# The polynomial of the norms' inverse root: from VectorE to GpSimd in a one-core transformer kernel

## What is computed

```python
def l2norm(t):
    return t / jnp.maximum(jnp.linalg.norm(t, axis=-1, keepdims=True), 1e-12)

def attn_layer(x, Wqkv, qs, ksc, Wo):
    q, k, v = jnp.split(x @ Wqkv, 3, -1)          # each to 16 heads of 64
    q, k = l2norm(q) * qs, l2norm(k) * ksc
    ...                                            # rotary tables on q and k
    out = local_attention(q, k, v)                 # softmax over two windows of 32
    return out @ Wo

def ffn_layer(x, g, bln, W1, b1, W2, b2):
    mu = x.mean(-1, keepdims=True)
    var = ((x - mu) ** 2).mean(-1, keepdims=True)
    xn = (x - mu) / jnp.sqrt(var + 1e-05) * g + bln
    ...
for i in range(DEPTH):                             # 6 layers
    x = attn_layer(shift_tokens(x), ...) + x
    x = ffn_layer(shift_tokens(x), ...) + x
```

## Time and profile before

| | before |
|---|---|
| median of 3 runs | 1721.71 us (1720.7 to 1721.73) |
| span of the profiled execution | 1725.8 us |
| TensorE busy | 1585.1 us, 92% |
| VectorE busy | 1446.8 us, 84% |
| ScalarE busy | 1117.1 us, 65% |
| GpSimd busy | 1069.6 us, 62% |

### The profile page before, as it was taken

How to read it: one execution, slowest core, us unless ns; L and a number is a source line. 1 busy time by engine, 2 the same in 40 slices (tenths; PEclk the granted TensorE clock), 3 DMA queues, 4 the chain that set the end, 5 groups by cost and what they waited for, 6 DMA issues and landing times.

```text
span 1725.8 us, 77157 instructions
## 1 busy us (share of the span) xinstructions
PE 1585.1 (92%) x32762; PEld 1278.6 (74%) x32763; DVE 1446.8 (84%) x3173; ACT 1117.1 (65%) x2014; POOL 1069.6 (62%) x1040
## 2 busy tenths in 40 slices
PE   4569999899999998999999999999999999999987
PEld 2247877777878777778777788777777777877874
DVE  8978988888889887888888889888888888888862
ACT  4346776667667666677666666666766666776663
POOL 3656766666666665667566567476576575665640
PEclk8589999999999999999999999999999999999998
DMA  2111110201111211110211111211111111011110
GB/s 86 31 44 49 40 49 25 77 24 48 44 37 37 65 36 38 41 49 28 67 34 48 41 37 40 61 37 52 38 40 40 49 49 44 29 47 44 33 46 13
DMA packets 41084, 75.06 MB, mean 43 GB/s; under 512 B 9472, under 2 KB 22568, under 8 KB 40744
## 3 DMA queue, kind: packets, MB, share of 16 engines
q1 hardware_dynamic: 40744, 70.12, 14.0%
HBM read 20.08 MB, written 2.10 MB: 13 GB/s over the span
## 4 chain that ended last, share of the span: by engine, by line
PE 75%; issue 9%; DVE 5%; ACT 4%; POOL 2%; ACTq 0%; DVEq 0%; POOLq 0%
PE bank L1359 8%; PE bank L1328 8%; PE bank L1465 8%; PE bank L1396 8%; PE wide L1436 7%; PE bank L1330 7%; PE bank L1329 7%; PE bank L1451 5%; PE bank L1529 4%; PE bank L1414 3%; PE bank L1385 2%; PE bank L1514 2%; PE bank L1515 1%; PE bank L1516 1%; PE bank L1476 1%
## 5 line engine op out<-in xcount | busy, mean ns | idle before, releaser
L864 POOL TENSOR_TENSOR qk<-qk,rnorm 128x512 f32<-128x512 f32 x384 | 401.8, 1046 | 351.0 <-DVE rnorm L1017 351.0
L856 POOL TENSOR_TENSOR qk<-qk,qk_sin 128x512 f32<-128x512 f32 x384 | 492.3, 1282 | 174.6 <-DVE qk_sin L978 174.5
L1180 ACT ACTIVATE squares<-bank 128x512 f32<-128x512 f32 x384 | 229.5, 598 | 152.6 <-DVE qk_sin L978 152.6
L988 DVE TENSOR_REDUCE norm<-squares 128x8 f32<-128x512 f32 x384 | 258.4, 678 | 30.7 <-ACT squares L1180 28.5
L1328 PE MATMUL bank<-w_hi,xs_hi 128*128 128x512 f32 x576 | 264.3, 459 | 12.3 <-ACT squares L1180 7.0
L971 DVE TENSOR_TENSOR qk<-bank,tables 128x512 f32<-128x512 f32 x384 | 261.6, 681 | 9.4 <-PE bank L1330 9.2
L978 DVE TENSOR_TENSOR qk_sin<-bank,tables 128x512 f32<-128x512 f32 x384 | 261.1, 680 | 0.6 <-POOL qk L856 0.6
L1330 PE MATMUL bank<-w_hi,xs_lo 128*128 128x512 f32 x576 | 230.3, 400 | 0.9 <-issue 0.9
L1329 PE MATMUL bank<-w_lo,xs_hi 128*128 128x512 f32 x576 | 229.2, 398 | 1.2 <-issue 1.1
L1359 PE MATMUL bank<-ident,qk 128*128 128x128 f32 x1536 | 226.5, 278 | 3.3 <-POOL qk L864 1.5
L1359 PEld LDWEIGHTS bank<-ident,qk 128*128 128x128 f32 x1536 | 181.0, 142 | 43.5 <-issue 5.0
(11 more groups left out here) (181 smaller groups left out, 2735.8 us busy)
## 6 DMA issues: line engine op xcount, KB each, us to landing
v<-v SPq DMA_DIRECT2D x96, 390.0 KB, 3.5
v<-v SPq DMA_DIRECT2D x72, 130.0 KB, 3.7
w_raw<-in_L_ffn_Wqkv SPq DMA_DIRECT2D x36, 256.0 KB, 3.9
w_o_s<-in_L_ffn_Wo SPq DMA_DIRECT2D x6, 512.0 KB, 5.9
w_raw<-in_L_ffn_W SPq DMA_DIRECT2D x6, 341.0 KB, 4.2
mix_x_nat<-in_L_attn_x SPq DMA_DIRECT2D x4, 256.0 KB, 3.5
w_raw<-x_res_scratch SPq DMA_DIRECT2D x4, 256.0 KB, 3.5
out<-w_raw SPq DMA_DIRECT2D x4, 256.0 KB, 3.1
```

What stands on the lines that cost most here:

```text
L856: pool.tensor_tensor(qk[:, g % 2, c, :], qk[:, g % 2, c, :], qk_sin[:, (QK_CHUNKS * g + c) % SINES, :], ALU.add).then_inc(added[c], 1)
L864: pool.tensor_tensor(view, view, rnorm[:, g % 2, c * HPC:(c + 1) * HPC].unsqueeze(2) .to_broadcast([P, HPC, DH]), ALU.mult).then_inc(norme ...
L988: dve.tensor_reduce(norm2[:, c * HPC:(c + 1) * HPC], squares[:, c % 2, :].rearrange("p (h d) -> p h d", d=DH), AX.X, ALU.add).then_inc(sum ...
```

## The change

The clamp and the seed stay on VectorE (`root_seed`, two instructions, the second raises the new semaphore `root_seeded`). The polynomial goes to GpSimd (`root`), at the start of its step, ahead of `normalise(step - 1, 3)`. GpSimd's three-input form is not used, so the seven instructions become ten: seven `tensor_tensor` and three `tensor_scalar`, with a semaphore wait between any two. The last raises `rooted`. `sum_squares` of chunk 0 now also waits for `rooted`, since it overwrites what the root reads.

```diff
+            chain = Chain(pool, late.pool_seq, late.pool_steps)
+            def root(g):
+                if not with_norms(g) and not with_var(g):
+                    return
+                x, y = norm2[:, root_cols(g)], rnorm[:, g % 2, root_cols(g)]
+                s, w = root_t[:, root_cols(g)], root_w[:, root_cols(g)]
+                pool.wait_ge(root_seeded, root_count(g))
+                chain(pool.tensor_tensor(s, x, y, ALU.mult))
+                chain(pool.tensor_tensor(w, s, y, ALU.mult))
+                chain(pool.tensor_scalar(s, w, 1.0, -10.0 / 3.0, ALU.mult, ALU.add))
+                chain(pool.tensor_tensor(s, s, w, ALU.mult))
+                chain(pool.tensor_scalar(s, s, 1.0, 5.0, ALU.mult, ALU.add))
+                chain(pool.tensor_tensor(y, s, y, ALU.mult))
+                chain(pool.tensor_tensor(s, x, y, ALU.mult))
+                chain(pool.tensor_tensor(w, s, y, ALU.mult))
+                chain(pool.tensor_scalar(w, w, -27.0 / 1024.0, 9.0 / 16.0, ALU.mult, ALU.add))
+                pool.tensor_tensor(y, w, y, ALU.mult).then_inc(rooted, 1)
...
+                root(step - 1)
                 normalise(step - 1, 3)
                 add(step - 1, 2)
...
                 dve.wait_ge(squared[c], g + 1)
+                if c == 0:
+                    need(dve, rooted, g)
...
                 seq(dve.tensor_scalar(x, x, 1e-24, None, ALU.max))
-                seq(dve.tensor_scalar(y.bitcast(I32), x.bitcast(I32), -0.5, float(0x5F3759DF), ALU.mult, ALU.add))
-                seq(dve.tensor_tensor(s, x, y, ALU.mult))
-                seq(dve.tensor_tensor(w, s, y, ALU.mult))
-                seq(dve.scalar_tensor_tensor(s, w, -10.0 / 3.0, w, ALU.add, ALU.mult))
-                seq(dve.scalar_tensor_tensor(y, s, 5.0, y, ALU.add, ALU.mult))
-                seq(dve.tensor_tensor(s, x, y, ALU.mult))
-                seq(dve.scalar_tensor_tensor(w, s, -27.0 / 1024.0, y, ALU.mult, ALU.mult))
-                dve.scalar_tensor_tensor(y, w, 9.0 / 16.0, y, ALU.add, ALU.mult).then_inc(rooted, 1)
+                dve.tensor_scalar(y.bitcast(I32), x.bitcast(I32), -0.5, float(0x5F3759DF), ALU.mult, ALU.add).then_inc(root_seeded, 1)
...
-                root(step - 1)
+                root_seed(step - 1)
                 rotate(step, 0)
```

More of the change, by code:

```diff
@@ L343, in _ @@
                 newton(b - 1)
+            late.pool_steps = seq.count
         @block.vector
@@ L486, in _ @@
             dve.wait_ge(xl_ready, BATCH - 1)
+            late.dve_steps = seq.count
         @block.scalar
@@ L757, in root_count, with with_norms, with_var, root_cols @@
             return g + 1 if live(g) else BLOCKS + 1
+        def with_norms(g):
+            return live(g)
+        def with_var(g):
+            return g == 0 or (g % NBLK == NBLK - 1 and real(g // NBLK - 1))
+        def root_cols(g):
+            return slice(0 if with_norms(g) else NORMS, NORMS + NBLK if with_var(g) else NORMS)
         def bank_of(c):
```

25 lines of the change are left out of this document (12 added, 13 removed).

## The result

The changed kernel takes 1806.8 us (median of 4 runs, 1802.77 to 1808.1). The kernel before, run beside it, takes 1721.2 us (4 runs, 1719.81 to 1721.73). The ratio is 1.0484, 95% interval 1.0467 to 1.0501. The forecast was 1788, range 1755 to 1840. The profiled execution spans 1806.3 us where before's spanned 1725.8, so the traces differ by 80.5.

What follows compares the result with a forecast made beforehand. TensorE was taken as the bound, waiting for a later root. 34.5 (t = 0) + 25 (t = 1 to 3) + 9 (ends of layers) + 1.4 (tail) - 4 (given back) = 66 us on 1721.7: 1788 us, range 1755 to 1840.

Steps and rivals of the forecast that it cites:

- rival (a): Faster, because VectorE was the bound and 152 us of work leave it: some 10 us gained, 1712 us; chance 0.05.
- Rival (b): No change: the root is late, but buffers and interruptions amid the score hide it, 1722 us; chance 0.04.
- rival (c): Slower by TensorE's direct waits alone, chain at 2.8 us: 35 us, 1757; chance 0.17 with the gap up to the forecast.
- rival (d): Slower by much, GpSimd's chain near 4.1 us: 137 us, 1859; by the page's ratio 155 us, 1877; chance 0.06.
- K1: Steps t = 1, 2, 3: TensorE's matmul delayed through chunk 1's sine part; 4, 12 and 9 us, 25 in all.
- tail: One root of 4 columns on the last path, behind the blocks: 1.4 us later.
- I take 1.5: Steps t = 0, where `widen_rstd` waits directly for the root: 1.5 us late in 23 items, 34.5 us.
- five such places x 1.8: Ends of layers, where GpSimd is full: root 3.4 us late instead of 1.6, 9 us in all.
- GpSimd has the time: it waited 4.86 us: GpSimd's wait before the root, read in one step, was taken as room for the added chain of 3.20 us.
- Given back: 4 us: Waits at `widen_rstd` precede the score, so interruptions there are partly waited out: 4 us subtracted, a chosen figure.
- TensorE's busy time as before: Sign expected in the profile after: TensorE's busy time unchanged, only its waits grown.
- VectorE idle some 3 us before the sine part, 96 times: Sign expected in the profile after: VectorE waiting before chunk 1's sine part, 3 us each, ended by GpSimd's addition.

Runs made afterwards that it cites:

- c5: The changed kernel with the polynomial's second round left out, five GpSimd operations plus the root's raising product gone; output not the kernel's; 1714.76 us, ratio 0.9969.
- late5: Against the changed kernel: VectorE makes the whole root, GpSimd passes it on through five dependent multiply-by-one operations before raising it; 1792.37 us, ratio 1.0397.
- add2: The changed kernel with GpSimd's addition of chunk 2 moved ahead of the root; 1776.84 us, ratio 1.0317.
- b_idle: The kernel before, with ten dependent idle operations on GpSimd ahead of its first normalisation in each step, root still on VectorE; 1744.24 us, ratio 1.0134.
- both: The changed kernel with the variance's four columns on VectorE and GpSimd's order addition of chunk 2, root, normalisation; 1742.3 us, ratio 1.0116.
- both_b: The changed kernel with the variance's four columns on VectorE and GpSimd's order root, addition of chunk 2, normalisation; 1742.09 us, ratio 1.0115.
- b_add2: The kernel before with only the addition of chunk 2 moved ahead of the first normalisation on GpSimd; 1731.95 us, ratio 1.0054.
- c15: The changed kernel with five more dependent operations (multiply by one, add zero) behind the ten on GpSimd; 1976.58 us, ratio 1.1471.

## Why the prediction was right, and where its sum was off

**Direction, mechanism and bound: right.** TensorE bounds, the root's lateness is what counts for most of the loss, the relief of VectorE comes back to almost nobody. c5 puts the relief at 6 us with the root on time (rival (a) had 10), late5 at little or nothing with the root late. Rival (b) falls with 23 waits of 1.67 us; rival (c), the direct waits alone, with the steps with t = 1, 2 and 3, whose 31 us add2 gives back; rival (d), with the ratio of the Trainium skill, GPSIMD Engine Reference, "Performance versus the Vector engine", falls with operations of 0.254 us: the chain measures 3.17 us (599.84 to 603.01), where 3.20 was taken and 4.4 would have followed from the ratio of 1.96.

**The sum, term by term** (profiled executions, from the table above):

| | predicted | measured |
|---|---|---|
| t = 0, with the ends of layers, less what is given back | 34.5 + 9 - 4 | 43.3, and 5.4 of t = 3's |
| K1 at t = 1 | 4 | 3.5 |
| K1 at t = 2 | 12 | 13.1 |
| K1 at t = 3 | 9 | 14.8; the five steps at ends of layers have 8.4 of it, 5.4 more than 5 x 0.59 |
| tail | 1.4 | 2.4 |
| ahead of the blocks | 0 | 3.4 |
| sum | 66 | 80.5 |

- `widen_rstd`, "I take 1.5": undisturbed steps with t = 0 grew by 1.0 to 1.4 us (17.38 to 18.42 in step 24, 17.05 to 18.41 in step 88), 1.3 in the median of those with no weight splits near. Nearly right, by 23 x 0.2 = 4 us too much.
- K1: undisturbed steps grew by 0.50 (t = 1), 1.33 (t = 2) and 0.80 (t = 3), where 0.29, 1.13 and 0.59 were worked out: 0.2 too little in each. In step 30, K1 itself is 1.04 late; 0.10 come from the matmul that no longer overlaps with the one before it, and the rest behind `turn_qk`, where the merge starts another 0.2 later. This term was counted in idle time, and a wait costs more. That the interruptions hide about half was right.
- Ends of layers, "five such places x 1.8": the two steps around them lost 18.5 us in all; without what such steps lose anyway (5 x 1.4 + 5 x 0.8 = 11), 7.5. Right in size, not in the way: against the first projection of its own step the root is 1.5 us late there (elsewhere 1.6 to 1.8), and not 3.4 as was worked out. It is the seed that grew (1.20 us), not the clamp, whose mean over all steps fell from 284 to 240 ns; and `turn_qk` waited 1.3 to 1.8 us for the normalisation, five times.
- Missing from the sum: the mid-layer weight splits. "GpSimd has the time: it waited 4.86 us" was read from one kind of step. In the ten steps behind those splits it had waited 1.9 us; they lost 19.8 us, 8.8 more than such steps lose anyway, as much again as the ends of layers. Some of this is the clock: three of the ten have a stretch of 3.4 us at 0.50.
- "Given back: 4 us" is a term that failed. It was chosen, not worked out. The interruptions amid the score came to 41.7 us in the blocks, 40.5 before: the waits ahead of the score used up none of them.
- Missing from the sum: the clock. The blocks have 13.6 us more at a granted clock of 0.50; at half speed that is up to 6.8 us. "TensorE's busy time as before" was wrong for two reasons, the clock and the overlap that a wait ends: it went from 1585.1 to 1605.2.
- "VectorE idle some 3 us before the sine part, 96 times": wrong in the form. It waits 1.76 us in step 30, since the early first rotation, too, must now wait for TensorE's projection (76.6 us in 83 steps). The moment at which the sine part starts was right to 0.1 us (5.92 us behind the seed's start forecast, 5.81 measured).
- The range: "half the way to (d)" would be 1824, from 1788 and 1859; the stated end of 1840 lies further out.

With 0.2 us more in 60 steps, nothing given back and the clock, the sum is 66 + 12 x 0.6 + 4 + 7 = 84 (the 0.6, a choice, for the steps that an interruption covers), against 80.5 and 85.6. The 4 us too much at `widen_rstd` and what the mid-layer splits cost beside the clock, some 4, about cancel. This was put together behind the result and tests nothing; that the forecast of 66 came as near as it did is in part luck, since terms left out were offset by others.

**Occupancy was a real rival, for a part.** b_idle loses 23 us with a root that is on time, both and both_b 20 us with both paths cut (in both, nearly). These losses lie mostly at the ends of layers and where weights are split. The trace shows two ways there: GpSimd comes out of the ten operations later than the root is ready, and VectorE's clamp and seed are held up by GpSimd's operations. b_add2 shows the second alone, 10 us, and all of it behind the mid-layer splits. How the 20 us are shared between the two was not separated. They don't add to the changed kernel's 86 as a separate sum: there, the root is late at the same places anyway. 65 us of paths and 20 us of the rest make 85 by construction, since the 20 is what both and both_b left; and add2's t = 0 shows that the parts interact.

**The rule that follows.** In the one order of operations, the time by the root's lateness: 0.06 us (c5) -6; 1.51 (late5) +70; 1.67 (changed) +86; 3.17 (c15) +254. Between 1.5 and 3.2 each further microsecond costs some 110 us: 96 steps, and the clock. These are four kernels, and they differ in GpSimd's number of operations too. With another order it doesn't hold: in both_b the first normalisation comes 2.80 us late (4.64 us behind the seed's start), and the kernel is 20 us slower.

**Left open.** What the interruptions in the score are: in the profiled executions they came to 32 to 42 us in the steps 4 to 94, with no order that the edits explain (32 in add2, 33 in both, 35 in c5, 42 in the changed kernel). So no single difference of a few us between two traces should be read as an effect of an edit. A fourth buffer for the sines, which would cut the path to K1 without moving an operation, was not tried; the kernel's other tiles leave no room for it.

## What to carry to other kernels

Moving a chain of dependent small operations to an idle engine is judged by when its last result is there, not by whose busy time it lowers: look for the engines that wait for it directly, then for the buffers that its followers free, two or three links further on, and multiply by the number of steps. Before VectorE's relief is counted as a gain, ask which of TensorE's waits the relieved work ends: here the root ended 3.4 us in 1500. Look at the helper's slack in every kind of step, not in one: here GpSimd waited 4.86 us in one and 1.9 to 2.3 in fifteen steps of other kinds. And a helper engine's long operations should not stand where the other engine's small critical ones run.
